# GAT logits summed in one PSUM bank, GpSimd left with the roots alone, and one written list for the whole round

## The reference, cut to what matters

```python
x = layernorm(x + L0(x, adj))   # GCN, two dense layers, batch norms
x = layernorm(x + L1(x, adj))   # x1 = relu(ln((L_norm x) Wc + bc)) + x
                                # o = attention(x1) @ Wo + bo;  x2 = ln(x1 + o, g2, be2)
                                # ln(x2 + gelu(x2 W1 + b1) W2 + b2, g3, be3)
x = layernorm(x + L2(x, adj))   # two GCN layers, then LSTMs over windows of 1, 2, 3, 4 nodes
# L3, graph attention (GAT):
Wh = h @ W;  s1 = Wh @ a1;  s2 = Wh @ a2
e = s1[:, :, None] + s2[:, None, :]          # row part + column part
e = where(e >= 0, e, 0.2 * e)                # leaky relu, then mask and softmax
out = layernorm(h + softmax(e) @ Wh)
```

## Time and profile before

| | |
|---|---|
| runs of the kernel | median 2414.89 us of 3 (2409.31 to 2415.82) |
| profiled execution | 2414.36 us, span 2412.5 us |
| mean granted TensorE clock | 0.948 |
| busy over the span | PE 87%, weight loads 75%, DVE 69%, ACT 57%, POOL 16% |
| third stage | from about 252 us to the end |
| chain that ended last | PE 57%, DVE 13%, issue 12%, ACT 5%, POOL 2% |

### The profile page before, as it was taken

How to read it: one execution, slowest core, us unless ns; L and a number is a source line. 1 busy time by engine, 2 the same in 40 slices (tenths; PEclk the granted TensorE clock), 3 DMA queues, 4 the chain that set the end, 5 groups by cost and what they waited for, 6 DMA issues and landing times.

```text
span 2412.5 us, 56320 instructions
## 1 busy us (share of the span) xinstructions
PE 2108.8 (87%) x21445; PEld 1816.0 (75%) x21445; DVE 1676.3 (69%) x4767; ACT 1367.9 (57%) x3387; POOL 380.9 (16%) x400
## 2 busy tenths in 40 slices
PE   8979569898888989898989888898989898989886
PEld 5634458888787868787888778786878788888875
DVE  6779456767676766776676767676677667676844
ACT  4557335555555646565556555565656565555554
POOL 0000111112121212121121112121212112111200
PEclk9989789999999999999999999999999999999997
DMA  7867100000000000000000000000000000000000
GB/s 265 277 238 268 53 10 2 2 28 2 29 2 27 2 28 2 28 2 29 2 2 28 2 29 2 27 2 29 2 28 2 29 2 2 28 2 10 2 10 10
DMA packets 37903, 92.68 MB, mean 38 GB/s; under 512 B 2544, under 2 KB 27120, under 8 KB 33392
## 3 DMA queue, kind: packets, MB, share of 16 engines
q1 hardware_dynamic: 37616, 88.86, 10.7%
...
## 4 chain that ended last, share of the span: by engine, by line
PE 57%; DVE 13%; issue 12%; ACT 5%; POOL 2%; DMA 0%; DVEq 0%; POOLq 0%; ACTq 0%
PE ps L260 16%; PE ps L262 15%; PE ps L261 15%; PE ps L1063 4%; POOL rstd L1476 2%; DVE stats L1549 2%; PE ps L1132 1%; PE ps L1274 1%; DVE pool_mem L1686 1%; DVE x L1580 1%; PE ps L1045 1%; DVE pool_mem L1670 1%; DVE pool_mem L1689 1%; PE ps L1054 1%; ACT hl_b L1328 1%
## 5 line engine op out<-in xcount | busy, mean ns | idle before, releaser
L1384 ACT ACTIVATE pool_mem<-ps,lstm_b 128x128 f32<-128x128 f32 (+2 forms) x1248 | 440.1, 411 | 329.6 <-PE ps L262 322.6
L260 PE MATMUL ps<-hl_a,w_hi 128*128 128x256 f16 (+2 forms) x1984 | 478.9, 264 | 59.4 <-DVE hl_a L1697 21.6
L261 PE MATMUL ps<-hl_a,w_hi 128*128 128x256 f16 (+2 forms) x1984 | 477.5, 264 | 0.0
L262 PE MATMUL ps<-hl_a,w_lo 128*128 128x256 f16 (+2 forms) x1984 | 477.2, 263 | 0.0
L1476 POOL TENSOR_TENSOR rstd<-ve,nhalf 128x2 f32<-128x2 f32 x224 | 182.7, 816 | 1404.9 <-DVE ve L1556 1404.9
L260 PE MATMUL ps<-hl_b,w_hi 128*128 128x168 f16 (+2 forms) x1408 | 354.6, 261 | 5.3 <-DVE hl_b L1697 3.8
L261 PE MATMUL ps<-hl_b,w_hi 128*128 128x168 f16 (+2 forms) x1408 | 354.6, 260 | 0.0
L262 PE MATMUL ps<-hl_b,w_lo 128*128 128x168 f16 (+2 forms) x1408 | 354.5, 260 | 0.0
L260 PE MATMUL ps<-pool_mem,w_hi 128*128 128x128 f16 (+2 forms) x1536 | 329.8, 241 | 21.3 <-DVE pool_mem L1691 21.2
L261 PE MATMUL ps<-pool_mem,w_hi 128*128 128x128 f16 (+2 forms) x1536 | 329.5, 241 | 0.0
L262 PE MATMUL ps<-pool_mem,w_lo 128*128 128x128 f16 (+2 forms) x1536 | 329.2, 240 | 0.0
...
## 6 DMA issues: line engine op xcount, KB each, us to landing
...
```

Source lines behind the costliest of these rows:

```text
L260: nc.tensor.matmul(o, l[0], r[0], start=first, stop=False, skip_group_check=True)
L261: nc.tensor.matmul(o, l[0], r[1], start=False, stop=False, skip_group_check=True)
L262: return nc.tensor.matmul(o, l[1], r[0], start=False, stop=last, skip_group_check=True)
L1384: op = nc.scalar.activation(gates[s][:, g, m * w:(m + 1) * w], ps[s][:, g, m * w:(m + 1) * w], ACT.Tanh, bias=lstm_b[:, bias:bias + 1], sc ...
```

## The change

- The row part of the GAT logits is made as wide as the column part: `wa1` holds the vector repeated 128 times, and 12 matmuls of 128 columns add it into the same bank, behind the 6 of the column part. The sign is put into the weights. ACT writes 0.2 of the bank to SBUF in one activation, and DVE takes the minimum of that and of the bank itself. The DVE step s1 is gone, and ACT waits for TensorE alone.
- bo and b2 are added by TensorE: one more matmul (a row of ones against the bias, `abias`, in fp16 parts on two partitions) behind each block of `attn_out` and `mlp_down`. `x1_bias` and `x2_bias` are gone; DVE adds x1 instead of xb.
- `xa_bias` is an addition on DVE, in place in xa (`shift_xa`), placed behind `norm_g1`. SP loads the next x only once `norm_g3` has read xa.
- The multiplication by the inverse sums is done by DVE, inside `exps`, behind the reciprocals.
- POOL keeps the roots.
- `ORDER` and `beside` are replaced by `ROUND`, one list for the whole round, in which the two half rounds have orders of their own and every entry names its stream ("0:" this round's tile, "0+" the next one's). Opening and closing are the "+" entries and the others, alone.
- New waits: `add_y` waits until ACT has read t of the tile before (`gat_ok.before(..., "out")`); the output store waits behind both streams' loads on SP.

```diff
+ROUND = """
+0:cell7 1:norm_g2.1 0+norm_y 0:hid7 0:inp8 1:mlp_up.0 1:gelu_split.0 1:turn_x2.1 0:cell8 1:mlp_down.0 0:hid8
+1:norm_g3.0 1:mlp_up.1 1:gelu_split.1 1:norm_l1.0 0:inp9 0:cell9 0:hid9 1:mlp_down.1 1:norm_g3.1 0:inp10 1:mix0.0
+0:cell10 0:hid10 1:norm_l1.1 1:gcn0.0 0:turn_state.0 1:mix0.1 1:mix1.0 0:norm_l2.0 0:turn_state.1 1:gcn0.1 0:turn_xc.0
+0:norm_l2.1 1:gcn1.0 0:gat.0 0:gat_exps.0 0:turn_xc.1 1:mix1.1 0:turn_att.0 0:gat_mix.0 0:gat.1 0:gat_exps.1
+0:norm_l3.0 0+turn_y.0 1:gcn1.1 0:turn_att.1 1:inp0 1:cell0 0+norm_l0.0 1:hid0 0:gat_mix.1 1:inp1 1:cell1 0+cheb.0
+1:hid1 0:norm_l3.1 0+turn_y.1 0+conv.0 1:inp2 1:cell2 0+norm_g1.0 0+norm_l0.1 1:hid2 1:inp3 0+xa_bias.0 0+turn_x1.0
+0+cheb.1 1:cell3 1:hid3 0+v.0 1:pack3 0+conv.1 0+norm_g1.1 1+norm_y 0+q.0 0+k.0 1:inp4 1:cell4 0+scores.0 0+xa_bias.1
+0+turn_x1.1 0+exps.0 1:hid4 1:inp5 0+v.1 0+q.1 0+k.1 0+turn_probs.0 0+scores.1 1:cell5 1:hid5 1:inp6 0+exps.1 1:cell6
+1:hid6 0+attend.0 1:pack4 0+turn_probs.1 0+attn_out.0 0+norm_g2.0 1:inp7 1:cell7 0+attend.1 1:hid7 1:inp8 0+turn_x2.0
+0+attn_out.1 0+norm_g2.1 0+mlp_up.0 0+gelu_split.0 1:cell8 0+turn_x2.1 0+mlp_down.0 1:hid8 0+mlp_up.1 0+gelu_split.1
+0+norm_g3.0 1:inp9 1:cell9 1:hid9 0+mlp_down.1 1:inp10 0+norm_l1.0 0+norm_g3.1 1:cell10 0+norm_l1.1 1:hid10 0+mix0.0
+1:turn_state.0 0+mix0.1 1:turn_state.1 1:norm_l2.0 1:norm_l2.1 0+gcn0.0 0+gcn0.1 1:turn_xc.0 0+mix1.0 1:turn_xc.1
+1:gat.0 1:gat_exps.0 1:gat.1 1:turn_att.0 1:gat_exps.1 0+mix1.1 1:gat_mix.0 1:turn_att.1 0+gcn1.0 1:norm_l3.0
+1:gat_mix.1 0+gcn1.1 1+turn_y.0 0+inp0 0+cell0 1+norm_l0.0 0+hid0 0+inp1 0+cell1 1+cheb.0 0+hid1 1+conv.0 1:norm_l3.1
+1+norm_g1.0 1+turn_y.1 1+norm_l0.1 0+inp2 1+xa_bias.0 0+cell2 1+turn_x1.0 0+hid2 0+inp3 1+cheb.1 1+v.0 1+conv.1
+1+norm_g1.1 1+xa_bias.1 0+cell3 1+turn_x1.1 0+hid3 0+pack3 1+q.0 1+k.0 1+v.1 1+q.1 0+inp4 0+cell4 0+hid4 1+k.1
+1+scores.0 1+exps.0 0+inp5 0+cell5 0+hid5 1+turn_probs.0 1+scores.1 1+exps.1 0+inp6 0+cell6 0+hid6 1+attend.0 0+pack4
+1+turn_probs.1 1+attn_out.0 1+norm_g2.0 1+attend.1 0+inp7 1+turn_x2.0 1+attn_out.1
 """.split()
...
 # dense(): one matmul more behind each block, also for "wo" and "w2"
+                        if with_row is not None:
+                            mm = nc.tensor.matmul(tok(s, bank)[:, b, :], with_row[0], with_row[1], start=False, stop=True,
                                                   skip_group_check=True)
...
 # gat_dense()
-                            mm = product(ps[s][:, BANK_B[h], HTOK + b:HTOK + b + 1],
+                            mm = product(ps[s][:, BANK_B[h], b * P:(b + 1) * P],
                                          (src[:, 0, k, a:a + P], src[:, 1, k, a:a + P]),
-                                         (wa1[:, 0, k:k + 1], wa1[:, 1, k:k + 1]), k == 0, k == KT - 1)
+                                         (wa1[:, 0, k, :], wa1[:, 1, k, :]), False, k == KT - 1)
...
 # ScalarE, gat_logits()
-                    act.wait_ge(*logit_ok.at(s, n, h, "s1"))
-                    for b in range(HALF):
-                        op = nc.scalar.activation(logit[s][h][:, b, :], ps[s][:, BANK_B[h], b * P:(b + 1) * P], ACT.Identity,
-                                                  bias=s1[s][h][:, b:b + 1], scale=-UNSCALE)
-                    op.then_inc(gat_ok.of(s, h), 1)
+                    act.wait_ge(*gat_ps.at(s, n, h, "logits"))
+                    nc.scalar.activation(logit[s][h], ps[s][:, BANK_B[h], 0:HTOK].rearrange("p (b n) -> p b n", b=HALF), ACT.Copy,
+                                         scale=0.2 * UNSCALE).then_inc(gat_ok.of(s, h), 1)
...
 # VectorE
+                        dve.wait_ge(*smax_ok.at(s, n, h, f"inverse{b}"))
+                        nc.vector.tensor_tensor(prob[s][h][:, b, :, :], prob[s][h][:, b, :, :],
+                                                ssum[s][:, i:i + HEADS].unsqueeze(2).broadcast_to([P, HEADS, P]), ALU.mult)\
+                            .then_inc(prob_ok.of(s, h), 1)
...
+                def shift_xa(s, n, h):
+                    dve.wait_ge(*feat_ps.at(s, n, h, "xp"))
+                    dve.wait_ge(*x_ok.at(s, n, h, "x1"))
+                    nc.vector.tensor_tensor(xa[s][:, blocks(h), :], xa[s][:, blocks(h), :], half_row("be3"), ALU.add)\
+                        .then_inc(pre_ok.of(s, h), 1)
...
 # VectorE, gat_logits()
-                    nc.vector.tensor_scalar(s1[s][h], ps[s][:, BANK_B[h], HTOK:HTOK + HALF], -UNSCALE, None, ALU.mult)\
-                        .then_inc(logit_ok.of(s, h), 1)
                     dve.wait_ge(*gat_ok.at(s, n, h, "logits"))
-                    nc.vector.scalar_tensor_tensor(logit[s][h], logit[s][h], 0.2, logit[s][h], ALU.mult, ALU.min)\
-                        .then_inc(logit_ok.of(s, h), 1)
+                    nc.vector.scalar_tensor_tensor(logit[s][h], ps[s][:, BANK_B[h], 0:HTOK].rearrange("p (b n) -> p b n", b=HALF),
+                                                   UNSCALE, logit[s][h], ALU.mult, ALU.min).then_inc(logit_ok.of(s, h), 1)
```

More of the change, by code:

```diff
@@ L84 @@
-mix1.0 gcn0.1 gcn1.0 mix1.1 gcn1.1 inp0 cell0
-""".split()
-ORDER = """
-hid0 inp1 norm_y turn_y.0 cell1 norm_l0.0 hid1 turn_y.1 cheb.0 norm_l0.1 inp2 conv.0 cell2 cheb.1 norm_g1.0 hid2 inp3
-conv.1 turn_x1.0 norm_g1.1 cell3 v.0 turn_x1.1 hid3 q.0 x1_bias.0 pack3 k.0 v.1 inp4 cell4 scores.0 hid4 inp5 exps.0
-q.1 x1_bias.1 k.1 cell5 turn_probs.0 scores.1 hid5 attend.0 inp6 exps.1 attn_out.0 cell6 norm_g2.0 turn_probs.1 hid6
-pack4 attend.1 turn_x2.0 inp7 cell7 attn_out.1 norm_g2.1 hid7 x2_bias.0 mlp_up.0 gelu_split.0 inp8 turn_x2.1 xa_bias.0
@@ L105, in opening @@
 def opening():
[L106 to L111 removed]
+    return [(name, s, 1) for s, after, name in ROUND if after]
 def parts(n):
@@ L122, in closing @@
 def closing():
-    return beside((0, ROUNDS), (1, ROUNDS)) + beside((1, ROUNDS), None)
+    return [(name, s, ROUNDS) for s, after, name in ROUND if not after]
 CELLS = [(1, 0, 0), (1, 0, TILE // 2)]
```

120 lines of the change are left out of this document (47 added, 73 removed).

## The result

The changed kernel takes **2288.97 us** (median of 4 runs, 2284.88 to 2292.63) where the kernel before took 2414.39 beside it. The ratio is 0.9484, 95% interval 0.946 to 0.9507: 5.2% faster, 125 us, three and a half times the 35 us that I forecast and outside my range. The profiled execution took 2291.22 us, 123 less than the one before.

A forecast was written before the change was run, and what follows sets the result against it. TensorE was taken as the bound, with 43 us of each 260.0 us round lost. 220.2 + 28.5 + 7 = 255.7 us per round, -4.3 times seven is -30, with the ends -35: 2380 us, range 2300 to 2445.

The forecast's parts named there:

- half speed and the rest: TensorE time per round lost at clock 0.50 and otherwise outside waits: 7 us instead of 11 (bounds 5 and 11).
- Floor: TensorE's own matmuls per round at unhindered spacing: 217.0 us plus 3.2 for added bias and logit columns, 220.2.
- Waits: TensorE's waits for its sources in one round: 28.5 us, against 32 before; wrong if above 32 or below 24.
- My own covers: TensorE work between a step and its source, set against the path's length: shortfalls of 14.3 us a round, loop head 3.5.
- the old list: The same queue calculation on the old order put turn_state 0.8 us too early, so 27.5 us became 28.5.
- the walk: Playing the list through DVE's and ACT's in-order queues: small delays add waits of 0.3 to 1.3 us, 27.5 in all.
- GpSimd's adds: Bias additions on GpSimd slowed two DVE scalings of x2 from 0.96 to 2.85 us; removal saves 1.9 us there.
- The multiplications on DVE: Multiplications by the inverse sums, moved from GpSimd into exps: each 0.35 us shorter than GpSimd's 1.04.
- The GAT logits: Path from TensorE's logits to turn_att: 0.7 us shorter (bounds 0.2 and 1.5), exponentials and table load staying on it.
- Ends: Outside the seven rounds: side-by-side parts -4 us, first half alone some -2.5, set-up +1.5, together -5.
- The covers are all that counts: Rival: small delays in DVE's queue do not add up; round 245 us, total 2300 us; chance 0.22.
- DVE's queue becomes the bound: Rival: DVE delays the LSTM chain at inp7 and turn_state; round 266 us, total 2460 us, slower; chance 0.22.

The follow-up runs named there:

- list_only: The kernel before, its biases, GpSimd multiplications and s1 step kept, played in the new list: 2319.1 us.
- gat_old: The changed kernel with the GAT logits as before (single-column row part, s1 on DVE, two activations): 2293.1 us.
- probs_pool: The changed kernel with the multiplications by the inverse sums back on GpSimd: 2292.0 us.
- extra_dve: The changed kernel with 16 added DVE multiplications a round whose result nobody reads: 2303.7 us.
- unrolled_wh_tp: The changed kernel without the loop and with Wh's copy behind the exponentials, plus pack4 moved behind turn_probs.1 in the list: 2257.1 us, against 2248.5 without that move.
- cheb_back: The changed kernel with norm_l0.0 and cheb.0 put back right behind turn_y.0 (turn_att.1 in the first half): 2412.3 us.
- unrolled_moves: The changed kernel without its loop, with three steps (turn_y.1, norm_l3.1, turn_state.0) moved in the list: 2312.8 us, against 2269.8 without these moves.

## Why the prediction was right in kind and wrong in size

The direction and the kind of mechanism held: in `list_only` the list is worth 96 us, through TensorE's waits and the half speed behind them. By the terms of the sum, against the count from start to start:

| us in one round | forecast | measured |
|---|---|---|
| TensorE's own work | 220.2 | 219.9 |
| waits | 28.5 | 18.3 |
| half speed and the rest | 7 | 6.5 |
| round | 255.7 | 244.7 |

- **Floor.** Right as a count. As a price (+3.2 in full, "none of it hidden") wrong: without the 1.7 us of bias matmuls the round is 244.7 us long, as with them.
- **Waits: the term that failed.** The forecast round was 11.0 us too long, 10.2 of them here; 18.3 is also below the 24 at which I had called myself wrong. My own covers had said 14.3 + 3.5 = 17.8. I then added 9.7 for delays in the queues and 1 for the old list.
- **What stood in the term's place.** `list_only`, with GpSimd's work still there, loses 24.6 us at waits, the changed kernel 18.3. So 6.3 of the 10.2 are paths that I took from the trace before, where GpSimd's work and the s1 hop stretched them, and which the change makes shorter: `gat_old` puts 1.4 of it on the GAT logits, `probs_pool` nothing on the multiplications, so that by elimination the additions have the rest. The other 3.9 are, by subtraction, the walk's own: `extra_dve` shows a seventh of added DVE time arriving. In the walk every late source counted; `unrolled_wh_tp` shows that a wait upstream is cover downstream.
- **The covers, place by place** (said, measured idle): `conv.0` 1.0 and 1.4, 1.0 and 2.0. `attn_out.0` 0.5, 0.7 in both halves. `turn_state` 1.6 and 2.2, 0.6 and 1.8. `turn_att` 1.9 and 0.6, 1.5 and 0.2. The loop 3.5, 2.5. But `inp7` 1.4 and 0.4, nothing; `turn_x2.0` 1.3, 0.3. Nothing above 1 us at `cheb`: right.
- **GpSimd's adds: mis-sized.** I priced 1.9 us at one moment from the earlier trace rows and folded it into the walk. The groups above give 7.5 us of DVE time a round, some of it on the other stream's LSTM chain; the biases are worth 48 to 59 us in the old order. In the new list they hit less (x2's scaling 598 ns). I had one row and should have asked the grouped view for every shape whose mean was above its usual 482 or 425 ns.
- **The multiplications on DVE**: "each 0.35 us shorter". They are (692 ns), and it is worth nothing (`probs_pool`), or less than that in the old order.
- **The GAT logits.** 0.7 us off the path: from TensorE's last logit to `turn_att` it was 5.16 us (1117.84 to 1123.00) and is 4.35 (1194.75 to 1199.10), 0.8 less. Right. But "the exponentials and their table load stay on it" was taken as given, and 17 us lay there. DVE's leaky relu from PSUM takes 424 ns, 425 from SBUF before: nothing, as booked. The 62 cycles that the Trainium skill (VectorE: DVE Perf Modes, The TRN2 errata) puts between the two sources don't show.
- **Half speed.** 7 us for it and the rest said, 6.5 measured, but not as I had it. I took half speed for most of 11 us a round from one round's clock of 0.97, and expected 4 us less. It was 9.3, went down to 1.6, and gave 7.7; the rest, 3.9, rose to 4.9. The stretches follow waits, as said, but "more, but shorter" waits cost far less clock than I thought.
- **Ends** -5 said, -12.6 measured; the set-up's part is as said (the stage's first transpose is 1.4 us later).
- **The rivals.** "The covers are all that counts" (2300 us, round 245, chance 0.22) is what happened, to within the ends. Against it stood only the walk. That its 17.8 came so near 18.3 is in part luck: the places that it names idle some 3 us less than it said, the loop 1 less, and some 3 us idle at places that it doesn't name (`attend.1` 1.0, `turn_x1` 0.5). "DVE's queue becomes the bound" would need `inp7` and `turn_state` to be late; even with 8.8 us more on DVE this costs 15 us in all. Yet cheb_back and unrolled_moves show the same mechanism at full strength one edit away.

Open is how much of the list's 96 us belongs to each of its moves: `cheb` alone costs 123 us when it is moved back, more than the whole list brought, so they don't add. And open is why GpSimd's additions cost most (59 us) when the multiplications are on DVE.

The fastest version is `unrolled_wh`: the changed kernel without the loop and with Wh's copy behind the exponentials, 2248.5 us, 6.9% below the kernel before and some 40 us below the changed one.
